# Blending the channel-mix input ahead of the receptance products, for five of the nine feed-forward units

## The reference, cut to what matters

```
x_prev = x shifted by one token (zeros ahead of the first)
xr = mu_r * x + (1 - mu_r) * x_prev
xk = mu_k * x + (1 - mu_k) * x_prev
r  = sigmoid(xr @ W_r.T)
k  = xk @ W_k.T
out = r * (relu(k)**2 @ W_v.T)
```

## Time and profile before

| | |
|---|---|
| runs, median (range) | 243.73 us (243.07 to 243.78) |
| the profiled execution, its own time | 243.37 us |
| its span, first to last instruction | 241.5 us |
| granted TensorE clock, mean over the span | 0.969 |
| PE, DVE, ACT, POOL busy | 89%, 84%, 74%, 58% |

### The profile page before, as it was taken

How to read it: one execution, slowest core, us unless ns; L and a number is a source line. 1 busy time by engine, 2 the same in 40 slices (tenths; PEclk the granted TensorE clock), 3 DMA queues, 4 the chain that set the end, 5 groups by cost and what they waited for, 6 DMA issues and landing times. The chain is left out here.

```text
span 241.5 us, 6529 instructions
## 1 busy us (share of the span) xinstructions
PE 214.8 (89%) x1962; PEld 161.2 (67%) x1962; DVE 204.0 (84%) x646; ACT 179.7 (74%) x696; POOL 140.9 (58%) x243
## 2 busy tenths in 40 slices
PE   0896897599999999999999999999999999999930
PEld 0893442357677767768876886887687768757920
DVE  1789999987977997885999899989989996965880
ACT  2366866739988688877978799779779977969671
POOL 7344043756667778756667675867575765545430
PEclk9999799979999999999999999999999999999985
DMA  5990000000000000000000002000100100010123
GB/s 116 231 291 7 3 0 0 1 0 4 3 1 4 0 3 0 4 1 3 0 5 0 3 1 48 3 0 3 45 4 0 29 18 4 1 43 3 43 51 91
DMA packets 10199, 6.45 MB, mean 27 GB/s; under 512 B 864, under 2 KB 9856, under 8 KB 10160
## 3 DMA queue, kind: packets, MB, share of 16 engines
q1 hardware_dynamic: 10016, 5.77, 9.8%
q0 software_dynamic: 144, 0.21, 0.4%
HBM read 3.88 MB, written 2.10 MB: 25 GB/s over the span
## 5 line engine op out<-in xcount | busy, mean ns | idle before, releaser
L958 PE MATMUL bank<-x,sg 64*64 64x256 f32 x256 | 35.5, 397 | 0.0
L660 ACT ACTIVATE bank<-bank,rsn 128x512 f32<-128x512 f32 x32 | 21.1, 659 | 18.1 <-PE bank L859 18.1
L958 PE MATMUL bank<-xg,sg 64*64 64x256 f32 x256 | 33.4, 380 | 0.0
L1371 DVE TENSOR_TENSOR x<-bank,wx 128x512 f32<-128x512 f32 x32 | 21.8, 682 | 12.5 <-ACT bank L660 12.0
L946 PE MATMUL pair<-x,turned_bc 64*64 64x256 f32 x224 | 31.2, 398 | 0.0
L425 POOL TENSOR_TENSOR x_lo<-xnT_all,x_hi 128x128 fp32r<-128x128 f32 x32 | 14.8, 462 | 21.1 <-ACT x_hi L575 21.0
L453 POOL TENSOR_TENSOR rb<-mse,halfn 128x2 f32<-128x2 f32 x32 | 25.2, 788 | 2.5
L1054 PE MATMUL bank<-wo_sb,yt 128*128 128x128 f32 x128 | 22.8, 300 | 0.0
L495 POOL TENSOR_TENSOR frs<-fmo,halfn 128x8 f32<-128x8 f32 (+2 forms) x13 | 15.1, 1158 | 13.2 <-DVE fmo L1463 13.2
L649 ACT ACTIVATE junk<-bank 128x64 f32<-128x64 f32 x64 | 13.9, 228 | 11.8 <-DVE bc L1354 9.6
L958 PEld LDWEIGHTS bank<-xg,sg 64*64 64x64 f32 x256 | 18.1, 135 | 6.7 <-issue 0.7
(11 more groups left out here) (193 smaller groups left out, 726.5 us busy)
## 6 DMA issues: line engine op xcount, KB each, us to landing
x_all<-x SPq DMA_DIRECT2D x16, 128.0 KB, 3.9
out<-o_all SPq DMA_DIRECT2D x14, 128.0 KB, 2.4
cm<-consts SPq DMA_DIRECT2D x1, 640.0 KB, 6.2
w_sb<-w_in SPq DMA_DIRECT2D x1, 480.0 KB, 4.2
out<-o_all SPq DMA_DIRECT2D x4, 64.0 KB, 2.1
cm<-consts POOLq DMA_DIRECT2D x1, 128.0 KB, 4.0
wo_sb<-w_out SPq DMA_DIRECT2D x1, 128.0 KB, 4.7
bcb_sb<-bc_bias SPq DMA_DIRECT2D x1, 96.0 KB, 4.3
```

Of the source, the lines that this page charges most:

```text
L660: nc.scalar.activation(x_ps[:], x_ps[:], ACT.Silu, scale=rsn[:, par:par + 1]).then_inc(S["x_silu"], 1)
L958: mm = nc.tensor.matmul(y_ps[par][half(h)], sg[half(h), a, r], rx(x, r)[half(h)], start=start, stop=stop)
L1371: vec.tensor_tensor((x1, xg)[a][:, par].rearrange("p (a e) -> p a e", e=P), x_ps[:].rearrange("p (a e) -> p a e", e=P), wx[:, par, a].unsq ...
```

## The change

For units 0 to 4 the tokens are blended before the product. ACT writes (1 - mu_r) * curT into a new buffer `behind`, at columns 1 to 64 of each sequence (`scaled_behind`, at the end of the K step); POOL moves column 64 into column 0 ahead of the next chunk (`carry_behind`, in the V step); DVE adds mu_r * curT to the first 64 columns of it and writes `mixed` (`mix`, in the R step, right behind `moments` and ahead of the next tile's x1). PE then makes each receptance tile from one product of `mixed` with the plain weights. Units 5 to 8 and all keys keep their two products. One more memset is issued on POOL at the start.

```diff
+MIX_UNITS = 5
...
+            nc.gpsimd.memset(behind[:], 0.0).then_inc(S["st_zero"], 1)
...
+            def carry_behind(c):
+                pool.wait_ge(C["mixed"], c)
+                nc.gpsimd.tensor_tensor(behind[:, :, 0:1], behind[:, :, L:L + 1],
+                                        one[:].unsqueeze(1).broadcast_to([128, B, 1]), ALU.mult).then_inc(C["first"], 1)
...
+                if q == 1 and 1 <= c - 2 < MIX_UNITS:
+                    carry_behind(c - 2)
...
+            def scaled_behind(u):
+                act.wait_ge(C["tr_sb"], u + 1)
+                wait_past(act, C["first"], u)
+                if u == 0:
+                    act.wait_ge(s_mix, 1)
+                nc.scalar.activation(behind[:, :, 1:], curT[:, sequences(u)], ACT.Identity, scale=one_less_mu[:, 0:1])\
+                    .then_inc(C["behind"], 1)
...
+                if q == 3 and 0 <= c - 2 < MIX_UNITS:
+                    scaled_behind(c - 2)
...
+                if u < MIX_UNITS:
+                    pe.wait_ge(C["mixed"], u + 1)
...
-                    nc.tensor.matmul(r_ps, cur[:, at_i], w_cur[:, 1], start=True, stop=False)
-                    mm = nc.tensor.matmul(r_ps, prev[:, at_i], w_prev[:, 1], start=False, stop=True)
+                    if u < MIX_UNITS:
+                        mm = nc.tensor.matmul(r_ps, mixed[:, k * 128:k * 128 + 128], wr_sb[:], start=True, stop=True)
+                    else:
+                        nc.tensor.matmul(r_ps, cur[:, at_i], w_cur[:, 1], start=True, stop=False)
+                        mm = nc.tensor.matmul(r_ps, prev[:, at_i], w_prev[:, 1], start=False, stop=True)
...
+            def mix(u):
+                dve.wait_ge(C["behind"], u + 1)
+                wait_past(dve, C["r_ps"], u)
+                vec.scalar_tensor_tensor(out=mixed[:].rearrange("p (b l) -> p b l", l=L), in0=curT[:, sequences(u)],
+                                         scalar=mu_sb[:, 0:1], in1=behind[:, :, 0:L], op0=ALU.mult, op1=ALU.add)\
+                    .then_inc(C["mixed"], 1)
...
                 if q == 0 and valid(c - 2):
                     moments(c - 2)
+                if q == 0 and 0 <= c - 3 < MIX_UNITS:
+                    mix(c - 3)
```

More of the change, by code:

```diff
@@ L286, in build @@
         prevT = sb("prevT", 128, 2 * B, L)
+        behind = sb("behind", 128, B, L + 1)
+        mixed = sb("mixed", 128, B * L)
         w_cur = sb("w_cur", 128, 2, D)
@@ L292, in build @@
         ff = sb("ff", 128, 2 * NQ, D)
-        cnames = ("x1 stats agg mom pow norm_bias normed tr_ps tr_sb carried shifted k_ps k_relu k_act r_ps th "
+        cnames = ("x1 stats agg mom pow norm_bias normed tr_ps tr_sb carried shifted behind first mixed k_ps k_relu k_act r_ps th "
                   "v_ps f stats3 res outv").split()
@@ L499, in carry @@
                 if c == 0:
-                    pool.wait_ge(S["st_zero"], 2)
+                    pool.wait_ge(S["st_zero"], 3)
                 pool.wait_ge(C["tr_sb"], c)
@@ L796, in ffn @@
                     outputs(c - 4)
-            act.wait_ge(S["st_zero"], 2)
+                if q == 3 and 0 <= c - 2 < MIX_UNITS:
+                    scaled_behind(c - 2)
+            act.wait_ge(S["st_zero"], 3)
             for n in range(-2, NT):
@@ L966, in state_part @@
                 else:
-                    pe.wait_ge(S["st_zero"], 2)
+                    pe.wait_ge(S["st_zero"], 3)
                     pe.wait_ge(t_turn[1], 3)
@@ L1594, in tiles @@
                 last_ffn(general)
-            dve.wait_ge(S["st_zero"], 2)
+            dve.wait_ge(S["st_zero"], 3)
             fl = dve.value_load(flag_i[0:1, 0:1], min_val=0, max_val=1)
```

## The result

The changed kernel takes 240.35 us (median of 4 runs, 240.20 to 241.12), the kernel before beside it 243.75 us (median of 4). The ratio is 0.9871 with a 95% interval of 0.9851 to 0.9891, a gain of 2.7 to 3.6 us. The forecast was 241.0 us, a gain of 2.76, at the lower edge of that interval. The profiled executions took 243.37 and 240.43 us, 2.94 us apart.

The account below looks back on a forecast made before the run. PE was taken to set the 22.35 us chunk period, DVE close behind. 4.45 us saved less 1.69 of stalls leaves 2.76: 243.73 - 2.76 = 241.0 us, range 239.2 to 242.9 (forecast's own 240.0 to 241.8).

Parts of the forecast that it names:

- PE sets the period, and 0.89 us go per unit: Receptances on PE: 22.35 us per chunk, all busy; one product per tile saves 0.89 us per unit, 4.45 in all.
- The blending at 0.65 us, hidden in chunk 3: DVE's `mix` in the R step: 0.65 us start to start, free in chunk 3's 0.68 us of idle time.
- DVE's shifts: DVE against the earlier trace, after blending and idle time: -0.96, -1.14, -1.32 us in chunks 4 to 6.
- PE's lead of 0.55 us over DVE before it stalls: K steps: PE can gain 0.55 us over DVE, then stalls 0.27, 0.71, 0.71 us in chunks 4 to 6.
- The sum: Whole kernel: 4.45 us saved on PE less 1.69 us of stalls leaves 2.76 us.
- What was costed at nothing: ACT's `scaled_behind` (about 0.62 us), POOL's `carry_behind` (0.21 us), the memset and the waits for `behind` and `mixed`: all covered.
- The tail: Units 5 to 8 stay as before and pass the gain on; DVE waits 1.53 us before unit 5's values.
- The rivals: Four other outcomes: full gain 0.19, `mix` held by POOL 0.17, DVE pacing slower 0.06, no effect 0.08.
- The full gain: PE's lead is larger or DVE's collisions with POOL get fewer: all 4.45 us kept, 239.3 us; chance 0.19.
- The held `mix`: POOL holds DVE's blending each time, 1.12 us: about 1.3 us of gain left, 242.5 us; chance 0.17.
- DVE pacing slower than before: DVE paces the chunks, slower than PE did: at 1.70 us per `mix`, 244.8 us; chance 0.06.
- That formula: With m us per `mix`, PE ends at 4m - 5.74; from m = 1.44 us slower than before.

Follow-up runs that it names:

- run with the o copy first: Changed kernel with ACT taking its copy of the next step's output projection out of PSUM ahead of normed and outputs: 240.53 us.
- run with ACT alone: Changed kernel with one product of unshifted tokens, no blending, no POOL column; ACT's scaling stays without a reader: 239.28 us.
- run with all helpers: Changed kernel with all helper work kept, but every receptance tile again made of two products: 243.71 us.
- two edits: On the changed kernel: `fmo` moved to POOL in chunks 2 to 7, 239.27 us; or POOL adding halves that ACT scales, in place of DVE's blending, 238.86 us.
- kernel with six units: Kernel in which POOL adds the blended halves, with unit 5 blended too, its addition between factors(7) and rstd(7): 238.81 us.

## Why the prediction was right, point by point

- **PE sets the period, and 0.89 us go per unit**: right. 0.81 us for the receptances of a unit, and 4.5 us in all where nothing else is added.
- **The blending at 0.65 us, hidden in chunk 3**: 0.66 us in chunks 4 to 7. In chunk 3 it took 1.20 us: there `fmo` (107.20) started 0.26 us ahead of POOL's scaling of the state and was not held to its end, and the blending, starting at 107.44, within 0.02 us of the scaling at 107.46, was. That `fmo` of chunk 5 "has waited that instruction out" was read rightly: eight columns wide it takes 0.17 us where nothing holds it (211.01 in the changed kernel). I had argued from chunk 5's rows and not looked at chunk 3's; that chunk had room for it.
- **DVE's shifts**: the step was right in kind, its room mis-sized. The prediction has -0.96, -1.14 and -1.32 at the V steps of chunks 4 to 6. Measured at x1: -1.06 (135.49 against 136.55), -1.44 (157.48 against 158.92) and -1.84 (179.46 against 181.30). DVE gains 0.38 and 0.40 us per chunk, not 0.18. I took idle times from the end of one instruction to the start of the next. Where DVE runs through, the next starts some 0.08 us ahead of the end (151.47 + 0.74 is 152.21, x1 starts at 152.13), so each gap is 0.08 us more than its figure: 0.81 and 0.21 in place of 0.73 and the 0.1 that I counted, 1.0 in place of 0.83. That is 0.19 of the 0.2 us.
- **PE's lead of 0.55 us over DVE before it stalls**: wrong. The lead is nil. PE's V step of chunk 5 starts at 155.23, 1.95 us ahead of before, and that of chunk 6 at 177.23, 2.33 us ahead; without the 0.89 us of their own receptances this leaves -1.06 and -1.44 behind the K step of the chunk ahead, and these are DVE's -1.06 and -1.44 of x1 to the digit. I had looked at two users, the turning of B and C and the state product, and not at the turning of y between them, which waits for ACT's o copy. In the trace of before that wait was already just met: 0.85 us behind L923, where it is 0.83 with nothing in the way. In chunk 2 of that trace, ahead of the rows that I read, it stands by name: L1045 at 97.01 waited 0.39 us for ACT's L688. The run with the o copy first shows that the next wait stands right behind it.
- **The sum**: the two misses cancel. Stalls came to 0.59 + 0.54 + 0.50 = 1.6 us where 1.69 were forecast, and 4.45 less that is 2.8 to 2.9. The traces are 2.94 us apart. It was luck that a room too small by 0.10, 0.20 and 0.22 us in the three chunks, together 0.52, met a lead too large by 0.55 us once.
- **What was costed at nothing**: right for ACT's scaling and POOL's column (the run with ACT alone at 239.28, the run with all helpers at 243.71).
- **The tail**: right. -2.75 at the last V step, -2.76 at the values of unit 5, which end DVE's wait at 220.66 in place of 223.42:

```profile
220.66 0.88 DVE L1513 SCALAR_TENSOR_TENSOR ff<-th,bank 128x128 f32<-128x128 f32 x4 [1.52 <-PE bank L1154]
```

- **The rivals**: none came. The full gain was 0.19 likely and is what two edits reach that give DVE room, at 239.27 and 238.86. The held `mix` came in chunk 3 alone. For DVE pacing slower than before, 1.44 us per blending was named as the point; the run with two blendings (1.33 us together) ended at 0.9979, just below no change, in keeping with it. That formula holds the same two misses, which cancel in it too. POOL's power behind `fmo`, which the rival named, came too late to hold the blending: in chunk 5 it starts at 152.66, 0.45 us behind its end.

## What to carry to other kernels

When work is moved off the engine that sets the pace, add up the next engine's chain over a whole period before and after: the new period was the longer of the two here, to within 0.1 us (21.46 and 21.99 us), whatever the first engine gained. Try the helper on the engine with the most idle time even if it is slower at it: POOL at 1.18 us beat VectorE at 0.74. Whether another place in VectorE's own stream would have done as well was not tried. And do not read a gain at the place where it is made; follow it through one period, because the wait that takes it back may stand half a period later, at an instruction that the change never touched.

## What the runs showed of the hardware

- POOL's scalings and additions and VectorE's instructions with two SBUF inputs hold each other, in both directions. VectorE's residual that started 0.07 us behind POOL's addition took 1.53 us in place of 0.61 (the kernel with six units). A blending that started 0.11 us ahead of POOL's scaling of the state took its normal 0.71 us, and POOL's took 1.09 in place of 0.63. The Trainium skill (page "SBUF — State Buffer", section "SBUF: two separate sides") says that whoever starts first keeps the shared pair of ports for the whole instruction and the other is blocked; these rows agree with it in both orders. I had read it in the prediction as a risk for VectorE alone. In chunk 3 of the changed kernel the order can't be read: the blending is shown 0.02 us ahead of POOL's scaling and is the one that took longer (1.20 us).
- POOL's power did not hold VectorE, though it reads SBUF too. VectorE's rotation (L1385) has two SBUF inputs and stands within it in the R steps of chunks 4 to 7, and kept the 0.54 us that it has in steps without the power:

```profile
152.66 1.64 POOL L499 TENSOR_TENSOR frs<-fmo,halfn 128x8 f32<-128x8 f32 x1
153.59 0.54 DVE L1385 TENSOR_TENSOR rot<-bc,cs_all 128x384 f32<-128x384 f32 x1
```

  By that rule the rotation would have waited until 154.26, where POOL's next instruction starts. Spans on POOL are rough, and why the power doesn't hold is not shown.
- So the order of start decides who pays, and with it whether the hold costs anything: for POOL it was free, for VectorE it would have been some 0.4 us per chunk (1.13 against 0.74).
- VectorE's instructions that follow each other without a wait start about 0.08 us before the one ahead is shown to end, in the changed kernel in every chunk. Idle times read between rows are short by that.
